# Inverse standard deviations by logarithm, exponential and one Newton step instead of square root and reciprocal

## The reference, cut to what matters

```python
h = _L0_tok_ref(x, ...)                       # (128, 64, 64): 64 samples with 128 tokens x 64 channels in the kernel
h = h + _L0_attn_ref(_layernorm(h), ...)      # local + linear attention, then an MLP with gelu; two norms inside
h = h + _L0_ffn_ref(_layernorm(h), ...)       # 16 experts, top 2 of 16, output normalised
h = h + _L1_attn_ref(_layernorm(h), ...)      # 8 heads of 64
h = h + _L1_ffn_ref(_layernorm(h), ...)       # 32 small experts, the best one of 32

def _layernorm(x, axis=-1, eps=1e-05):
    m = jnp.mean(x, axis=axis, keepdims=True)
    v = jnp.var(x, axis=axis, keepdims=True)
    return (x - m) / jnp.sqrt(v + eps)
```

## Time and profile before

| | |
|---|---|
| three runs | 989.49, 986.7, 983.88 us (median 986.7) |
| profiled execution | 982.16 us, of which the span of the core's work is 980.4 us |
| mean granted clock of TensorE | 0.977 of full speed |
| stretches of attention and experts with half the full clock (1.2 in place of 2.4 GHz) | 163.3-170.1, 258.9-262.3, 313.5-316.9, 600.3-607, 624.2-627.5, 880.1-883.5 us |
| stages (start of each in the span) | tokenizer 0, attention0 158, mlp0 266, experts0 313, attention1 590, experts1 874 us |

### The profile page before, as it was taken

How to read it: one execution, slowest core, us unless ns; L and a number is a source line. 1 busy time by engine, 2 the same in 40 slices (tenths; PEclk the granted TensorE clock), 3 DMA queues, 4 the chain that set the end, 5 groups by cost and what they waited for, 6 DMA issues and landing times. The chain is left out here.

```text
span 980.4 us, 35512 instructions
## 1 busy us (share of the span) xinstructions
PE 924.4 (94%) x12674; PEld 670.1 (68%) x12674; DVE 702.7 (72%) x1964; ACT 642.8 (66%) x1205; POOL 518.7 (53%) x814
## 2 busy tenths in 40 slices
PE   7899988999798999999999997899999999969998
PEld 2355556777566888888888884566666666658887
DVE  4577745777666577877878778788888888875553
ACT  1245556888666677877878775777777777754444
POOL 0001015888684578787887875455555656452110
PEclk8899998999999999999999998999999999999999
DMA  8624000000000000000000000000000000000001
GB/s 281 110 34 64 0 2 1 2 0 0 2 1 1 3 3 3 0 0 0 0 0 0 1 3 1 1 3 0 0 0 0 0 0 0 1 2 18 21 21 28
DMA packets 10961, 14.89 MB, mean 15 GB/s; under 512 B 9392, under 2 KB 9520, under 8 KB 9968
## 3 DMA queue, kind: packets, MB, share of 16 engines
q1 hardware_dynamic: 10704, 13.63, 6.1%
q10 hardware_dynamic: 192, 0.39, 0.2%
HBM read 11.92 MB, written 2.10 MB: 14 GB/s over the span
## 5 line engine op out<-in xcount | busy, mean ns | idle before, releaser
L1807 ACT ACTIVATE e_hid<-ps,cst 128x512 f32<-128x512 f32 x256 | 155.1, 687 | 53.7 <-PE ps L1579 53.7
L1514 POOL TENSOR_TENSOR e_acc<-e_acc,e_part 128x512 f32<-128x512 f32 x96 | 122.2, 1273 | 34.1 <-DVE e_part L1735 27.1
L1591 PEld LDWEIGHTS ps<-ew,e_hid 128*64 128x64 f32 x4096 | 124.8, 138 | 21.9 <-issue 10.4
L1591 PE MATMUL ps<-ew,e_hid 128*64 128x64 f32 x4096 | 133.8, 224 | 0.0
L1579 PE MATMUL ps<-e_xs,ew 64*128 64x256 f32 x1024 | 129.7, 393 | 0.0
L1735 DVE TENSOR_TENSOR e_part<-ps,e_wt 128x512 f32<-128x512 f32 x128 | 86.8, 687 | 44.5 <-PE ps L1591 39.6
L1579 PEld LDWEIGHTS ps<-e_xs,ew 64*128 64x128 f32 x1024 | 94.6, 189 | 15.7 <-issue 2.7
L2004 POOL TENSOR_TENSOR a_sum<-a_part 128x256 f32<-128x256 f32 x64 | 46.5, 727 | 94.0 <-DVE a_part L2112 93.9
L2073 PEld LDWEIGHTS ps<-cst,a_ex 128*128 128x128 f32 x512 | 56.6, 143 | 50.7 <-issue 50.7
L2101 DVE TENSOR_REDUCE a_rmax<-ps 128x8 f32<-128x1024 f32 x64 | 78.1, 1221 | 14.9 <-PE ps L2065 13.0
L226 POOL TENSOR_TENSOR t_prob<-t_ex,t_rscale 128x512 f32<-128x512 f32 x8 | 11.9, 1491 | 133.2 <-DVE t_rscale L477 133.2
(11 more groups left out here) (258 smaller groups left out, 1994.0 us busy)
## 6 DMA issues: line engine op xcount, KB each, us to landing
x_in<-x_dram SPq DMA_DIRECT2D x42, 128.0 KB, 4.8
cst<-cst_dram SPq DMA_DIRECT2D x1, 3101.0 KB, 13.0
out_dram<-e_res SPq DMA_DIRECT2D x16, 128.0 KB, 2.0
ew<-ew_dram SPq DMA_DIRECT2D x1, 1024.0 KB, 15.1
cst<-cst_dram SPq DMA_DIRECT2D x1, 704.0 KB, 5.1
ew<-ew_dram SPq DMA_DIRECT2D x1, 512.0 KB, 16.9
x_in<-x_dram ACTq DMA_DIRECT2D x6, 64.0 KB, 3.7
x_in<-x_dram SPq DMA_DIRECT2D x6, 64.0 KB, 3.8
```

Of the source, the lines that this page charges most:

```text
L1514: eng.tensor_tensor(acc[:, :, :, :], acc[:, :, :, :], part[n % RING][:, :, :, :], ALU.add).then_inc(sum_sb.sem, 1)
L1591: mm = eng.matmul(m.ps[rows, 6 + n % 2, to:to + C], hid[e % 8][:, a:a + C], w2[:, e * C:e * C + C], start=True, stop=True)
L1807: nc.scalar.activation(hid[e % 8][:, :].rearrange("p (r t) -> p r t", r=2), m.ps[:, 4 - 2 * (n % 2):6 - 2 * (n % 2), j * 256:(j + 1) * 256 ...
```

## The change

The reciprocal of the square root becomes exp(-0.5 * ln(v + eps)) on ScalarE, followed by one Newton step on VectorE, y * (1.5 - 0.5 * (v + eps) * y * y). `Ln` and `Exp` lie in one set of tables, `natural_log_exp_and_others`, which is named explicitly where a set is preloaded. So each deviation is two activations with a wait between them, and each inverse is three `scalar_tensor_tensor`, each waiting for the one before, in place of one reciprocal. The late and the early part of n1 get one more instruction and a second refinement. In mlp0 the set is loaded and Gelu's set is loaded again behind each norm piece. Other stages keep their pieces where they were.

```diff
@@ tokenizer, act
-        eng.preload_act_table(ACT.Exp)
+        eng.preload_act_table_set(LOGS)
@@ norm, deviation
-            nc.scalar.activation(dev[:, sl], var[:, sl], ACT.Sqrt, bias=m.eps[:, :]).then_inc(std_sb, 1)
+            nc.scalar.activation(log[:, sl], var[:, sl], ACT.Ln, bias=m.eps[:, :]).then_inc(log_sb, 1)
             if twice:
-                nc.scalar.activation(dd[:, sl], var[:, sl], ACT.Sqrt, bias=m.eps2[:, :],
-                                     scale=1.0 + EPS).then_inc(std_sb, 1)
+                nc.scalar.activation(log2[:, sl], var[:, sl], ACT.Ln, bias=m.eps2[:, :],
+                                     scale=1.0 + EPS).then_inc(log_sb, 1)
+            eng.wait_ge(log_sb, per * n + 1)
+            nc.scalar.activation(dev[:, sl], log[:, sl], ACT.Exp, scale=-0.5).then_inc(std_sb, 1)
+            if twice:
+                eng.wait_ge(log_sb, per * n + 2)
+                nc.scalar.activation(dd[:, sl], log2[:, sl], ACT.Exp, scale=-0.5).then_inc(std_sb, 1)
+        def refine(eng, sl, first, v, shift, to, count):
+            eng.scalar_tensor_tensor(out=diff[:, sl], in0=first[:, sl], scalar=-0.5, in1=first[:, sl],
+                                     op0=ALU.mult, op1=ALU.mult).then_inc(root_sb, 1)
+            eng.wait_ge(root_sb, count + 1)
+            eng.scalar_tensor_tensor(out=m2[:, sl], in0=v[:, sl], scalar=shift, in1=diff[:, sl],
+                                     op0=ALU.add, op1=ALU.mult).then_inc(root_sb, 1)
+            eng.wait_ge(root_sb, count + 2)
+            eng.scalar_tensor_tensor(out=to[:, sl], in0=m2[:, sl], scalar=1.5, in1=first[:, sl],
+                                     op0=ALU.add, op1=ALU.mult).then_inc(ready, 1)
@@ norm, inverse
+            if twice:
+                eng.wait_ge(var_sb, n + 1)
+                eng.tensor_scalar(var2[:, sl], var[:, sl], 1.0 + EPS, EPS * EPS, ALU.mult, ALU.add).then_inc(own2, 1)
             eng.wait_ge(std_sb, per * n + 1)
-            eng.reciprocal(rstd[:, sl], dev[:, sl]).then_inc(ready, 1)
+            refine(eng, sl, dev, var, EPS, rstd, 2 * per * n)
             if twice:
+                eng.wait_ge(ready, used + 2)
                 eng.wait_ge(std_sb, per * n + 2)
-                eng.reciprocal(rstd2[:, sl], dd[:, sl]).then_inc(ready, 1)
+                eng.wait_ge(own2, n + 1)
+                refine(eng, sl, dd, var2, 0.0, rstd2, 2 * per * n + 2)
@@ mlp0, act
             if left == 0:
+                eng.preload_act_table_set(LOGS)
                 m.parts["n3"][1](eng, 0)
                 eng.preload_act_table(ACT.Gelu)
             if left == 2 and not back:
+                eng.preload_act_table_set(LOGS)
                 m.parts["n2"][1](eng, 1)
+                eng.preload_act_table(ACT.Gelu)
@@ experts0, dve
         def normal(g):
             eng.wait_ge(dev_sb.sem, dev_sb.at(g))
-            eng.reciprocal(y_rstd[:, :], y_dev[:, :]).then_inc(rstd_sb.sem, 1)
+            eng.scalar_tensor_tensor(out=y_root[:, :], in0=y_dev[:, :], scalar=-0.5, in1=y_dev[:, :],
+                                     op0=ALU.mult, op1=ALU.mult).then_inc(root_sb.sem, 1)
+            eng.wait_ge(root_sb.sem, root_sb.at(g, 1))
+            eng.scalar_tensor_tensor(out=y_root[:, :], in0=y_var[:, :], scalar=EPS, in1=y_root[:, :],
+                                     op0=ALU.add, op1=ALU.mult).then_inc(root_sb.sem, 1)
+            eng.wait_ge(root_sb.sem, root_sb.at(g))
+            eng.scalar_tensor_tensor(out=y_rstd[:, :], in0=y_root[:, :], scalar=1.5, in1=y_dev[:, :],
+                                     op0=ALU.add, op1=ALU.mult).then_inc(rstd_sb.sem, 1)
@@ experts0, act
         def deviation(g):
-            nc.scalar.activation(y_dev[:, :], y_var[:, :], ACT.Sqrt, bias=m.eps[:, :]).then_inc(dev_sb.sem, 1)
+            nc.scalar.activation(y_log[:, :], y_var[:, :], ACT.Ln, bias=m.eps[:, :]).then_inc(log_sb.sem, 1)
+            eng.wait_ge(log_sb.sem, log_sb.at(g))
+            nc.scalar.activation(y_dev[:, :], y_log[:, :], ACT.Exp, scale=-0.5).then_inc(dev_sb.sem, 1)
```

More of the change, by code:

```diff
@@ L38 @@
 SHUT = 2.0 ** 100
+LOGS = "natural_log_exp_and_others"
 HALVES = (slice(0, P // 2), slice(P // 2, P))
@@ L657, in make @@
     def make(nc, ctx, m):
-        diff, m2, dd, var, dev, tmp, mean, rstd, rstd2 = m.norm_tiles
+        diff, m2, dd, var, dev, tmp, mean, rstd, rstd2, log, log2, var2 = m.norm_tiles
         own = ctx.enter_context(nc.semaphore(f"{name}_parts"))
@@ L661, in make @@
         std_sb = ctx.enter_context(nc.semaphore(f"{name}_std"))
+        log_sb = ctx.enter_context(nc.semaphore(f"{name}_log"))
+        root_sb = ctx.enter_context(nc.semaphore(f"{name}_root"))
         ready = ctx.enter_context(nc.semaphore(f"{name}_ready"))
         m.norm_ready = ready
-        m.norm_value = 3 if twice else 2
+        m.norm_value = value = 3 if twice else 2
+        own2 = ctx.enter_context(nc.semaphore(f"{name}_var2")) if twice else None
         m.norm_late = m.norm_value * (2 if late else 1)
@@ L695, in inverse @@
         def inverse(eng, n=0):
             sl = samples[n]
+            used = value * n
+            if twice:
+                eng.wait_ge(var_sb, n + 1)
+                eng.tensor_scalar(var2[:, sl], var[:, sl], 1.0 + EPS, EPS * EPS, ALU.mult, ALU.add).then_inc(own2, 1)
             eng.wait_ge(std_sb, per * n + 1)
-            eng.reciprocal(rstd[:, sl], dev[:, sl]).then_inc(ready, 1)
+            refine(eng, sl, dev, var, EPS, rstd, 2 * per * n)
             if twice:
+                eng.wait_ge(ready, used + 2)
@@ L820, in attention0 @@
     xs = [sb(f"xs{b}", [P, HT]) for b in range(2)]
-    mean, rstd, rstd2 = m.norm_tiles[6:]
+    mean, rstd, rstd2 = m.norm_tiles[6:9]
     w_kv, w_q, w_tok = m.a0_weights
@@ L1447, in experts0 @@
     part_sb, sum_sb, y_stat = step("part_sb", NE), step("sum_sb", NE), step("y_stat", TS)
-    own_sb, var_sb, dev_sb, rstd_sb = step("own_sb", 4), step("var_sb", 2), step("dev_sb"), step("rstd_sb")
+    own_sb, var_sb, log_sb, dev_sb = step("own_sb", 4), step("var_sb", 2), step("log_sb"), step("dev_sb")
+    root_sb, rstd_sb = step("root_sb", 2), step("rstd_sb")
     yc_sb, yn_sb, yg_sb, h_sb, h_stat = step("yc_sb"), step("yn_sb"), step("yg_sb"), step("h_sb"), step("h_stat", TS)
-    y_diff, y_sum, y_m2, y_dd, y_mean, y_var, y_dev, y_rstd = (
-        sb("y_" + n, [P, TS]) for n in ("diff", "sum", "m2", "dd", "mean", "var", "dev", "rstd"))
+    y_diff, y_sum, y_m2, y_dd, y_mean, y_var, y_log, y_dev, y_root, y_rstd = (
+        sb("y_" + n, [P, TS]) for n in ("diff", "sum", "m2", "dd", "mean", "var", "log", "dev", "root", "rstd"))
     yc, yn = sb("yc", [P, TS, C]), sb("yn", [P, TS, C])
@@ L2428, in audio_tower_kernel @@
         m.norm_tiles = [ctx.enter_context(nc.sbuf_tensor(f"norm_{n}", [P, S], F32)) for n in
-                        ("diff", "m2", "dd", "var", "dev", "tmp", "mean", "rstd", "rstd2")]
+                        ("diff", "m2", "dd", "var", "dev", "tmp", "mean", "rstd", "rstd2", "log", "log2", "var2")]
         m.a0_weights = [ctx.enter_context(nc.sbuf_tensor(n + "s", [P, P], F32)) for n in ("wkv2", "wq2", "wtok")]
```

## The result

| | median | runs | mean clock of TensorE |
|---|---|---|---|
| before, same chip | 985.09 us (983.53 to 989.49) | 5 | 0.977 in the profiled run |
| after | 991.56 us (990.72 to 993.95) | 5 | 0.966 to 0.970 |
| after, once more on a second chip | 988.98 us (986.6 to 994.06) | 12 | 0.972 on average |
| before, second chip | 987.25 us (983.6 to 991.61) | 29 | 0.972 on average |

The change makes the kernel slower: ratio 1.0061 (95% interval 1.004 to 1.0082) on the first chip, 1.0022 (1.0006 to 1.0038) on the second. The forecast was 995 with a range of 981 to 1001 on a median of 986.7, that is +8.3; measured are +6.5 and +1.7 on the medians. By the prediction's bound of 0.5% the first is "slower" and the second "same".

The account below looks back on a forecast made before the run. TensorE was taken as the bound, busy 924.4 of 980.4 us. Borders -2.1, Newton steps in experts0 +9.8 and norm parts there +1 gave +8.7; on the median of 986.7 that is 995 us, range 981 to 1001.

Parts of the forecast that it names:

- rival 1: In experts0, slack absorbs the Newton steps: 984.6 us, or up to 989 with stalls under 0.3 a round; chance 0.30.
- Table loads: On ScalarE, 36 of 44 loads go and 28 exponentials come: net 40.4 us less, nearly all off the path.
- Rival 2: Table loads gate experts0, so 11.6 us of TensorE's waits would go, to 973 us; chance 0.09.
- loads are hidden: At n2's and n3's early parts, loads cost nothing now, and the longer VectorE chain adds 0.3 us each.
- Borders: At six stage borders, TensorE's pauses near norm pieces change by -0.55 us, with the clock -2.1 together.
- Elsewhere GpSimd is too little occupied for it: Outside experts0, Newton steps were taken not to wait for GpSimd, so no such cost was counted.
- Clock: Behind the stage-border pauses, one spell of lower TensorE clock less: -1.5 us, bounds +1.5 and -3.
- Newton's steps in experts0's rounds: Three VectorE steps wait for GpSimd and stall TensorE 0.7 us in 14 steady rounds: +9.8 us; chance 0.50.
- my hand working: At `normal` in experts0, all three steps wait for GpSimd: L1675 ends 3.0 us later, `weighted(0)` begins 1.5 late.
- Norm parts in experts0: n3's late and n5's early part within experts0 add three Newton steps each: +1 us in all, 0 to 2.
- rival 3: Nothing lost in experts0, every border at its favourable end, two clock spells gone: 981.7 us; chance 0.06.

Follow-up runs that it names:

- direct: `tables` with ScalarE's exponential written straight where the inverse deviations are read, no VectorE reciprocal or Newton step; 979.14 us, ratio 0.9905 to the kernel before.
- e0only: Kernel before with only experts0 changed (logarithm, exponential, three Newton steps a round), norms between stages keeping square root and reciprocal; ratio 1.0102.
- tables: Changed kernel with all Newton steps left out, one VectorE multiplication by 1 in their place, inverse deviations unrefined; ratio 0.9948 to the kernel before.
- newton_borders: Changed kernel with Newton steps in experts0's rounds replaced by one multiplication by 1, those of the norms between stages kept; ratio 0.9994 to before.
- newton_e0: Changed kernel with Newton steps of the norms between stages replaced by one multiplication by 1, those in experts0's rounds kept; ratio 0.9952 to before.
- newton5: newton_e0 with two more two-input VectorE steps that change nothing in each experts0 round, five in all; ratio 1.0015 to the kernel before.
- n5_plain: Changed kernel with the refinement of n5's first 48 samples replaced by a multiplication by 1; ratio 1.0024 to the kernel before.
- chain3: `tables` with three dependent one-input VectorE multiplications in place of one in each experts0 round; ratio 0.9961 to the kernel before.
- control: Kernel before run once more without any edit; 987.33 us, ratio 1.0005.
- after2: Changed kernel run once more on a second chip without any edit; 988.98 us, ratio 1.0022 to the kernel before.

## Why the prediction was right or wrong

The direction held on both chips, and the times lie in the range; that the sum came close was in part luck. Its largest term, +9.8, was measured at about 1, and on the first chip 2.1 us of clock that I hadn't forecast, and a low median of before, filled some of the gap; on the second chip +1.7 were left of +8.3. By the test that the prediction set itself (steps of up to 1.3 us and rounds that stay at 17.2), rival 1 is right.

**Table loads.** Right: 8 loads are left, 36 gone, ScalarE at 602.4 us. Worth in experts0's rounds: 0.00 us (`direct`). Rival 2, -11.6 us by the waits for e_hid, is refuted: those waits are as long with no load there (10.3 us in the kernel after, 12.3 in `direct`). Behind a load the activation starts 0.02 us after its end (456.93 + 1.28, then 458.23, in e0only), so a load costs ScalarE 1.3 us. But "loads are hidden" holds only one at a time: e0only, with two close together, loses 9.9 us, of which its Newton steps are about 1.

**Borders.** Forecast -2.1, of it -0.55 for the work and -1.5 for the clock. The net of the work was about right: at equal clock the change is +2.5 to +3.0, experts0's stretch +2.8 of it, so the other stages net between -0.3 and +0.2, where I had -0.55. It is a difference of two larger terms: the tables alone gain 3.0 us (`tables`), and Newton's steps in the norms take back 3.6 to 4.2 (newton_borders), of which 1.1 in experts0. The pauses at n5, n2 and n3 came out to 0.1 us. n6 and n1 didn't: at n6 one wait was only exchanged for another. At n1 the steps also waited for GpSimd, which I had excluded with "Elsewhere GpSimd is too little occupied for it", and the 0.8 us won came back as a new pause of 2.0.

**Clock.** The step that failed is "I count one spell less: 4.05 - 5.60, -1.5 (bounds +1.5 and -3)". n5's pause shrank to 1.9 us, and the clock fell behind it all the same (0.57 in the window from 634.0). In the first five executions the clock gave +2.1 us (32.3 - 28 lost, at 0.49), beyond my upper bound, on the second chip nothing. The length of one pause doesn't tell what follows: n3's is 3.1 us in two executions of before, with 3.4 us at half clock behind it in one and 6.8 in the other, and 3.4 us in two of the changed kernel, with 10.3 and 6.8 behind it. The prediction also left out the half clock of before from 258.9 us, behind no pause longer than this:

```profile
258.15 0.44 PE L1065 MATMUL ps<-a_qsT,a_ctxm 128*64 128x128 f32 x4 [1.54 <-issue]
```

What does set the length stays open, and with it a part of why the two chips gave +6.5 and +1.7.

**Newton's steps in experts0's rounds.** The term that was mis-sized: "I take 0.7 for 14 steady rounds: +9.8". Measured are 0.7 to 1.1 us in the whole stretch (newton_e0 against `tables`; the two profiles of after without their last round). That steps wait for GpSimd was right, the lag was not, at two places. Against my hand working no round has all three steps waiting: in most two wait and one slips in right behind, in four only one waits. And the lag faded down the order, where I had it grow. In the round at 500 us L1711 ends at 503.54, 3.89 us after the round's reference (the start of e_wT at 499.65), where before it was 491.86 - 490.49 = 1.37: +2.5 for +3.0. `weighted(0)` began 0.94 us late for my 1.5 and `weighted(3)` 0.75 for 1.8. And `weighted(4)` was 0.67 us later against TensorE, not 1.6 to 1.9. With 0.84 us of slack the difference between these two numbers is nearly the whole term. Rival 1 is what happened in these rounds, in its form "with a stall of under 0.3 a round", and only in every second one; newton5 shows what my forecast looks like when the slack is used up.

**Norm parts in experts0.** Forecast +1 (0 to 2), measured +1.8 in the last round of the kernel after (18.63 for 16.83), 1.4 to 1.7 by n5_plain, all of it n5's first part: inside the bounds.

In short: forecast -2.1 + 9.8 + 1; at equal clock the runs show about 0 at the borders, 1.0 in steady rounds and 1.8 in the last. The time fell into the range because it was taken with both ends of an uncertain slack. By its own terms the range's upper end is 986.7 + 15.4 + 2 - 2.1 = 1002, not 1001, and its lower end of 981 is rival 3's time, not rival 1's; nothing hangs on either.

## What to carry to other kernels

Taking work off an engine that nobody waits for gains nothing there, whatever its size: 26 table loads in experts0 were worth 0.00 us, and the whole gain of `direct` lies outside experts0's stretch, where ten other loads went; no run separates them there from the reciprocals that went with them. Where a short VectorE chain runs beside a busy GpSimd, count a step that meets it at up to one whole GpSimd instruction, but not every step: here one or two of three waited. Compare the sum with the slack of the first consumer that TensorE waits for; the answer turns on tenths of a microsecond, so work the slack out at each later hand-over and let the range cover both sides. A shared table set pays only if every function of the region draws on it: half the change was slower than all of it, with loads in pairs where the functions of two sets met.

The version to keep is `direct`: logarithm and exponential on ScalarE alone, 0.9905 of the time before. It leaves out the refinement, and what that costs in accuracy no run here measures.

## What the runs showed of the hardware that I had not expected

- A VectorE TENSOR_SCALAR with one SBUF input waits for a running GpSimd instruction (median 1178 ns, up to 1203, in chain3; 147 at least) like one with two, and so does a single one in `tables` (mean 782); a RECIPROCAL of the same shape at the same place doesn't (163 at most).
- Three dependent steps beside three GpSimd instructions in a row never all wait. In the kernel after, the first and the third wait in ten of 16 rounds (1.01 and 1.19 us at 500 us, the second 0.16) and only the second in four (1.25 us at 448 us, the others 0.15 and 0.16); chain3 has both kinds of round too.
- The mean granted clock of one kernel differs between executions (0.970 to 0.974 in twelve of the control, 0.967 to 0.981 in twelve of after2), and each us lost to the lower clock goes with about half a us of time.
